# First FFN of a three-block kernel: transposes moved ahead of products, one normalisation on VectorE, key and value rounding on GpSimd

## The reference, cut to what matters

```
x = x + 0.5 * ffn(layernorm(x))
x = x + attention(layernorm(x))
x = x + 0.5 * ffn(layernorm(x))
```

```
h          = square(relu(up(x * score)))          # per chosen expert, bf16
routed_out = down(h)
shared_out = square(relu(x @ shared_up.T)) @ shared_down.T    # fp32
out        = routed_out summed over the 2 choices + shared_out
```

## Time and profile before

| what | value |
|---|---|
| median of 3 runs | 713.45 us (712.92 to 713.6) |
| the profiled execution's own time | 712.66 us |
| its span in the profile | 710.6 us |
| PE busy | 644.7 us, 91% |
| DVE busy | 533.0 us, 75% |
| ACT busy | 470.7 us, 66% |
| POOL busy | 285.5 us, 40% |
| first FFN, to the first reduction of scores | 0 to 121.1 us |
| second FFN, from its first shared product | 621.4 us to the end |

### The profile page before, as it was taken

How to read it: one execution, slowest core, us unless ns; L and a number is a source line. 1 busy time by engine, 2 the same in 40 slices (tenths; PEclk the granted TensorE clock), 3 DMA queues, 4 the chain that set the end, 5 groups by cost and what they waited for, 6 DMA issues and landing times.

```text
span 710.6 us, 9499 instructions
## 1 busy us (share of the span) xinstructions
PE 644.7 (91%) x3009; PEld 453.5 (64%) x3024; DVE 533.0 (75%) x1048; ACT 470.7 (66%) x893; POOL 285.5 (40%) x354
## 2 busy tenths in 40 slices
PE   3898988769999999999999999999999989889997
PEld 2444443557777777777777776777777777645542
DVE  3799876757867787677686877767777885799885
ACT  3577887546675665766766667666666556478886
POOL 4655412043534434254252443425433547642200
PEclk9899999989999999999999999999999999999999
DMA  7011100225043150422505224051340504000001
GB/s 280 2 37 54 59 30 0 65 55 119 15 104 81 40 119 8 112 66 55 119 1 118 57 63 104 15 119 36 85 107 13 119 9 110 1 0 31 30 15 45
DMA packets 24803, 44.39 MB, mean 62 GB/s; under 512 B 4955, under 2 KB 5555, under 8 KB 24627
## 3 DMA queue, kind: packets, MB, share of 16 engines
q1 hardware_dynamic: 24467, 43.78, 24.6%
q10 hardware_dynamic: 288, 0.01, 0.0%
HBM read 8.12 MB, written 2.10 MB: 14 GB/s over the span
## 4 chain that ended last, share of the span: by engine, by line
PE 40%; DVE 31%; ACT 15%; issue 9%; POOL 2%; SPq 1%; DMA 1%; ACTq 0%; DVEq 0%; POOLq 0%
DVE bank_max L929 10%; DVE E L881 8%; DVE p_lo L874 5%; ACT E L629 4%; PE banks L1175 4%; ACT probs L639 4%; PE banks L1055 4%; PE banks L1220 4%; PE banks L1222 3%; PE banks L1221 3%; PE banks L1064 3%; PE banks L1177 3%; PE banks L1176 3%; ACT p_hi L606 3%; DVE probsT L788 3%
## 5 line engine op out<-in xcount | busy, mean ns | idle before, releaser
L418 POOL TENSOR_TENSOR p_lo<-probsT,p_hi 128x512 fp32r<-128x512 f32 x128 | 164.3, 1289 | 286.6 <-ACT p_hi L614 286.6
L929 DVE TENSOR_REDUCE bank_max<-banks 128x1 f32<-128x512 f32 (+1 forms) x192 | 162.0, 853 | 23.4 <-PE banks L1177 21.0
L874 DVE TENSOR_TENSOR p_lo<-banks,p_hi 128x512 fp32r<-128x512 f32 x128 | 87.7, 685 | 97.0 <-ACT p_hi L606 96.8
L629 ACT ACTIVATE E<-banks,neg_max 128x512 f32<-128x512 f32 (+1 forms) x96 | 79.3, 830 | 91.8 <-DVE neg_max L954 86.2
L1175 PE MATMUL banks<-kv_lo,q_parts 128*128 128x512 f32 x256 | 113.9, 445 | 27.0 <-ACT probs L639 13.4
L639 ACT ACTIVATE probs<-banks,neg_max 128x512 f32<-128x512 f32 (+1 forms) x96 | 79.3, 830 | 73.3 <-DVE neg_max L954 73.3
L509 ACT ACTIVATE probsT<-probsT 128x1024 bf16<-128x1024 bf16 x96 | 92.3, 981 | 33.0 <-DVE probsT L788 24.3
L788 DVE SCALAR_TENSOR_TENSOR probsT<-banks,E 128x1024 bf16<-128x1024 f32 x80 | 95.5, 1219 | 22.5 <-PE banks L1055 19.6
L1220 PE MATMUL banks<-p_hi,kv_lo 128*128 128x512 f32 x256 | 107.9, 421 | 1.5 <-POOL p_lo L418 1.3
L1222 PE MATMUL banks<-p_hi,kv_hi 128*128 128x512 f32 x256 | 102.3, 400 | 0.0
L1221 PE MATMUL banks<-p_lo,kv_hi 128*128 128x512 f32 x256 | 102.0, 399 | 0.0
(11 more groups left out here) (101 smaller groups left out, 867.7 us busy)
## 6 DMA issues: line engine op xcount, KB each, us to landing
probsT<-E SPq DMA_DIRECT2D x256, 128.0 KB, 2.4
kv_stage<-in_keys_values SPq DMA_DIRECT2D x8, 512.0 KB, 3.5
out<-X SPq DMA_DIRECT2D x8, 256.0 KB, 2.0
X<-in_x SPq DMA_DIRECT2D x1, 1280.0 KB, 9.2
X<-in_x SPq DMA_DIRECT2D x3, 256.0 KB, 5.3
probs<-in_wup SPq DMA_DIRECT2D x1, 704.0 KB, 5.3
probs<-in_wdown SPq DMA_DIRECT2D x1, 704.0 KB, 6.6
sup_s<-in_shared_up SPq DMA_DIRECT2D x1, 88.0 KB
```

The costliest lines, as they stand in the source:

```text
L418: pool.tensor_tensor(moved_part(p_lo, ring), moved_pair(w, m), moved_part(p_hi, ring).bitcast(fp32), ALU.subtract).then_inc(moved_lo_done, 1)
L874: dve.tensor_tensor(own_part(p_lo, ring), own_squares(ring), own_part(p_hi, ring).bitcast(fp32), ALU.subtract).then_inc(p_lo_done, 1)
L929: dve.tensor_reduce(bank_max[:, i % 2, k:k + 1], score_banks(u, i)[:, first:first + count, :].rearrange("p b n -> p (b n)"), AX.X, ALU.max ...
```

## The change

In the prologue DVE normalises group 0 itself, and POOL does so from group 1 on. PE transposes the weights of group 0 behind the up product of slot 0 and ahead of the shared up products; ACT copies them out ahead of the shared relu. POOL, and no longer ACT, rounds each block of keys and values to `kv_hi`, directly ahead of its own subtraction. SP drops its wait on `kv_hi`, since `kv_lo` comes behind it.

```diff
@@ SP
             for b in range(2, KV):
-                sp.wait_ge(kv_hi_done, b - 1)
                 sp.wait_ge(kv_lo_done, b - 1)
@@ POOL
                         if g:
                             cast_xT(g - 1, g - 1, g - 1)
-                        normalize(g, g)
+                            normalize(g, g)
...
                     if f == 0:
+                        pool.wait_ge(kv_loaded[i % 2], (i // 2 + 1) * 16)
+                        pool.tensor_copy(kv_hi[:, i, :], kv_stage[:, i % 2, :]).then_inc(kv_hi_done, 1)
                         pool.wait_ge(kv_hi_done, i + 1)
                         pool.tensor_tensor(kv_lo[:, i, :], kv_stage[:, i % 2, :], kv_hi[:, i, :].bitcast(fp32),
                                            ALU.subtract).then_inc(kv_lo_done, 1)
@@ ACT
-            def split_kv(i):
-                act.wait_ge(kv_loaded[i % 2], (i // 2 + 1) * 16)
-                act.activation(kv_hi[:, i, :], kv_stage[:, i % 2, :], ACT.Copy).then_inc(kv_hi_done, 1)
...
                     if f == 0 and i == 0:
+                        copy_wbc(0, xT_bank)
                         shared_relu(G)
-                        copy_wbc(0, xT_bank)
                         copy_xT(2, 2, 2, xT_bank)
...
-                    if f == 0:
-                        split_kv(i)
@@ DVE
+            def normalize_first():
+                dve.wait_ge(rstd_done, 1)
+                for t in range(GT):
+                    last = dve.tensor_scalar(xn[:, t, :], X[:, t, :], neg_mean[:, t:t + 1], rstd[:, t:t + 1],
+                                             ALU.add, ALU.mult)
+                last.then_inc(normalized, 1)
...
                         moments_of(g, g)
+                        if g == 0:
+                            normalize_first()
@@ PE
                     up(G, 0)
+                    if f == 0 and i == 0:
+                        pe.wait_ge(xT_copied, 2)
+                        transpose_weights(0, xT_bank)
                     if i:
                         down(G - 1, 3)
                     shared_up_product(G)
...
                     if f == 0 and i == 0:
-                        pe.wait_ge(xT_copied, 2)
-                        transpose_weights(0, xT_bank)
                         pe.wait_ge(wbc_copied, 1)
                         transpose_for_ffn(2, 2)
```

## The result

| | before | after |
|---|---|---|
| median | 712.91 us (7 runs) | 710.16 us (7 runs, 707.85 to 711.43) |
| ratio | | 0.9963, 95% interval 0.9947 to 0.9979 |
| profiled execution, its span | 712.66, 710.6 us | 711.43, 707.8 us |

The change gains 2.75 us by the medians and 2.8 us by the spans. The profiled executions' own times differ by only 1.23 us, because the span after leaves out 3.6 us of its time and the one before 2.06.

A forecast was written before the change was run, and what follows sets the result against it. Three limits take turns: pipeline fill to about 42 us, PE (ACT close) in even groups, DVE from even to odd. Gains 2.0 + 0.56 + 0.76 = 3.3 us: 709.3 profiled, median 710.1; range 707.0 to 713.6.

The forecast's parts named there:

- The head: First FFN up to slot 0 of group 1: 2.0 us gained, half from earlier start, half from shorter hold; bounds 0.7 to 2.4.
- the spread weights: Group 0's spread weights ready at 17.1, a microsecond before PE needs them; without DVE's normalising they would just miss.
- the first relu: DVE's first weighted relu, group 0, starts at 19.7 instead of 22.57, 2.9 us earlier.
- so do its copy, its cast and the tiles of group 3: Head: these start 1.0 us earlier, like group 2's transposes; slot 3's up product moves from 30.05 to 29.1.
- better clock: Rival, head: PE stays at 2.4 GHz, slot 3 some 1.75 us earlier, 708.4 us; chance 0.17, shared with missed holds.
- DVE normalises group 0: Prologue: four tiles in 0.87 us (bounds 0.72 and 1.75); transposes, copy and logits of group 0 come 0.9 earlier.
- The hold in the head: Group 0: POOL's copy and subtraction pair ends at 33.2; DVE's two-input routing step loses 1.1 us instead of 2.1.
- ACT without the rounding: First FFN: 0.28 us gained in each of two even-to-odd stretches, 0.56 together, and 0.76 in the last stretch.
- POOL with the rounding: POOL, each group: rounding copy adds 1.05 us, fits in idle time; its next statistics are not delayed.
- the slower rival: Rival, POOL: rounding copy costs 2.35 us and holds DVE; 0.6 us lost, 714.05; chance 0.17.
- The hold in groups 2 and 4: DVE routing: loss stays 2.0 us, now at step L761 with slot 4 behind it; gain 0.
- a hold that is missed: Rival, groups 2 and 4: routing steps slip past POOL's work, 2.0 us each, down to 706.1; chance 0.17, shared with better clock.

The follow-up runs named there:

- head_only: The changed kernel, but ACT keeps the rounding of keys and values: 711.44 us, ratio 0.9979 against the kernel before.
- fill: The changed kernel with products nobody reads in two gaps of PE in the first FFN's head: 710.32 us, ratio 0.9959 against the kernel before.
- pool_norm: The changed kernel with group 0 normalised by POOL again: 710.55 us, ratio 0.9962 against the kernel before.
- copy_twice: The changed kernel with a second POOL copy of each block, into kv_lo, then overwritten: 711.72 us, ratio 0.9980 against the kernel before.
- again: The changed kernel once more, unaltered, in a later batch: 708.69 us, ratio 0.9931 against the kernel before.
- odd_pairs: The changed kernel, but POOL splits two blocks in each odd group and none in even ones: 705.34 us, ratio 0.9883 against the kernel before.
- odd_low: The kernel before, but POOL subtracts two blocks in each odd group, none in even ones; ACT still rounds: 708.36 us, ratio 0.9931.
- warm: The changed kernel with 26 unread transposes of the identity before the first x arrives: 710.87 us, ratio 0.9968 against the kernel before.
- kv_only: The kernel before with the rounding on POOL and SP's wait as in the change, head untouched: 712.02 us, ratio 0.9974.

## Why the prediction's time was right and its largest term was not, point by point

**The time.** 710.1 forecast, 710.16 measured; 3.3 us forecast as gained, 2.75 measured. That the two are so close is luck: one term was 1.4 too large, and the others were too small by 0.9 together (holds 0.4, a step between slots 0 and 1 of group 3 0.3, the rest of the kernel 0.2).

**The head, 2.0 forecast, 0.58 measured.** This is the term that was mis-sized. Its first steps were right: the spread weights were there in time, the first relu came at 19.76 (forecast 19.7), and normalising on DVE took 1.12 us (0.87 taken, bounds 0.72 to 1.75). The step that failed is "so do its copy, its cast and the tiles of group 3, whose transposes go from 26.33 to 25.3, and slot 3's up product, from 30.05 to 29.1": they went to 26.12 and 30.30. The 1.2 us missing there have three parts. The shared products ended at 22.06, not 21.3, so the transposes of group 2 started at 21.89 and won 0.63 us, not 1.0. On ACT the shared relu (22.09 to 23.11) now stood ahead of the copy of group 2, which started at 23.01 and so kept 0.20 of the 0.63. Together that is 0.8. And behind the transposes of group 3 PE took 4.18 us instead of 3.72, at 1.2 GHz for 10 us instead of 7: 0.46. I had carried the old clock over unchanged and kept a better clock as a rival only. The clock was no property of the edit: the shared products took 2.62 us in head_only, which has the same head, and fill shows what a clock that stays up does to slot 3: 28.9 instead of 31.36.

**DVE normalises group 0.** The price was right and the gain was not: pool_norm has the first relu at 19.50 without it. The forecast had the spread weights just miss without this edit. There they didn't: PE made the transposes at 17.68, straight behind the up product. The order of PE's work did all of it.

**The hold in the head, forecast as 1.0 shorter.** POOL was held up with the rest and subtracted from 31.58, not 30.8, and DVE met it two steps sooner, at L758 instead of L763. L758 is a tensor_scalar with one tensor input. The forecast had only two-input steps held; had it held this one as well, its own times (slot 3 done at 31.3, pair to 33.2) would have made the hold some 1.8 us and the head about 0.7 less, by my estimate. The step was 1.34 us too long (1.49 less the 0.15 that it takes unheld), against 2.1 before: 0.8 shorter. Less the 0.25 by which slot 3 was later, that is the 0.58.

**ACT without the rounding, 0.56 and 0.76.** Right, 0.29 and 0.27 in the stretches of groups 2 and 4, and 0.77 at the end, where 10.27 us stands as the second FFN had it.

**POOL with the rounding.** The copy took 1.04 us, forecast 1.05, and its next statistics were not delayed. copy_twice confirms the price of the slower rival: with 2.1 us of copying, 1.55 us are lost.

**The hold in groups 2 and 4, forecast as unchanged.** The place was right, L761 (now L763) instead of L742, three steps later; the gain of 0.19 and 0.20 is what the earlier start of POOL's pair takes off the 1.97. That slot 4 is late there and costs nothing was right as well: the shared product of group 3 starts at 60.14, later than the 59.68 of before, and slot 0 of group 3 is still 1.06 earlier. Gained beyond this: 0.3 us between slot 0 and slot 1 of group 3, which no term had; no run shows what gave them.

The Trainium skill, SBUF — State Buffer, section Who interferes with whom, says that a VectorE instruction with two SBUF inputs contends with a GpSimd instruction that reads SBUF, that a tensor_scalar in a mode that uses both ports does so too, and that whichever was issued first blocks the other in full. What I left open, whether a copy does it too, copy_twice and the 0.34 us step at 55.62 answer: it does, for both kinds of DVE instruction. The trace doesn't agree for every GpSimd instruction: beside POOL's four normalising ones at 24.30 (0.45 us each, which read `X` from SBUF) two-input steps took their usual 0.19 us. The measurement decides here, and it was made with POOL's instruction of 128x128 with two per-partition scalars only.

**The rivals.** The better clock, at 708.4, did not come in the two profiled executions of the changed kernel (that others had it, the mean clocks under again suggest); where it was forced (fill) it gave 0.9 and not the 1.75 that I had worked out, because the steps did not slip ahead of the pair, they ran into its copy. What I priced at 2.0 per group for a hold that is missed was near: from slot 3 to slot 0 odd_pairs takes 5.39 us, 1.83 less than before and 1.64 less than the changed kernel.

## What to carry to other kernels

- When an engine's tiny instructions take as long as another engine's big one, compare their ends before looking at either engine's load. Here a 0.2 us routing step on DVE was held by POOL's subtraction for 2 us in three places, and moving POOL's work to a group without such steps made the first FFN 6.2 us shorter (odd_low), where the three edits of this change made it 2.6 shorter.
- A gain at the start of a pipeline is only worth what the latest of its inputs leaves. A new order on PE and ACT won 2.8 us for the first relu, and with the other edits 0.6 remained for slot 0 of the next group. An edit whose result then waits for something else, as DVE's normalising did for the tiles of group 1, shows in no time at all. Ask, too, whether the stretch runs at PE's high clock, and take its price at both levels.
- A stall and a slow clock can cover each other. Removing only the second gave 0.9 us, on top of the first 3.5: try them together before either is given up.

## What the runs showed of the hardware that I had not expected

**PE's clock in the head.** Of the 11 profiled kernels without the unread products in the two gaps, ten had a stretch at 0.50 that began between 24 and 27 us and lasted 3, 7 or 10 us; head_only had none. The three with them had none. Ahead of the falls that I followed PE had been idle for 0.8 to 1.2 us, once in the changed kernel and twice in pool_norm and copy_twice. The Trainium skill, TensorE: Matmul & The Clock Gate, section What's actually happening, says that the clock follows how busy PE has been. The trace agrees in part: with the gaps filled the clock stayed up in three of three, against one of eleven without. The program alone doesn't settle it: head_only had PE idle for 0.69 and 1.05 us at these places and stayed at 1.00. What a low clock cost is slot 3 2.5 us later (changed kernel against fill).

**Transposes raise the clock.** After 26 transposes alone, the logits of group 0 took 1.03 us where they take 1.85 without (warm against the changed kernel); the trace's record of the clock has the rise at 5.57 us, while the transposes ran. The column of the granted clock says 1.00 in both. In the changed kernel it shows full speed from the start to 24.96 us, though the logits of group 0 take 1.85 us at 10.58 and those of group 2 take 1.06 at 23.65: at the start of an execution the durations have to be read.

**A clock that falls once near the end of the attention.** Where the part behind the first reduction took 591.1 us and not 589.5, the extra 1.6 lie between 568 and 581 us, with equal work and a lower clock. The kernel before has 1.00 in these stretches; kv_only has

```profile
560.00:570.00 10.00, 9.94 (x49) 1.00 0.32 74
570.00:580.00 10.00, 7.68 (x38) 0.86 0.00 0
580.00:590.00 10.00, 10.00 (x54) 0.97 0.36 82
```

PE is idle there for 2.3 of 10 us in both. Seven of the 14 profiled executions have the longer part, of kernels that don't differ in the attention, so I take it for a matter of the execution; no kernel was profiled often enough to show it within one. It is more than half of the effect studied here, which is why small changes of this kernel are better compared by events inside the first FFN.
